# Filler counts and lane turns of the last loop in a four-layer decoder kernel

## What is computed

```python
x = _layernorm(x + _L2_attn_ref(x, ...))          # gated convolution
x = _layernorm(x + _L2_xattn_ref(x, ctx, ctx, ...))  # cross attention 0
x = _layernorm(x + _L2_ffn_ref(x, rhs))           # per-token int8 product
x = _layernorm(x + _L3_attn_ref(x, ...))          # retention
x = _layernorm(x + _L3_xattn_ref(x, ctx, mask, ...))
# cross attention 1, self attention and a gelu MLP, each with a norm
x = _layernorm(x + _L3_ffn_ref(x, ...))           # ternary MLP
# its body:
h = silu(tlin(x, w1, w1_s)) * tlin(x, w2, w2_s)
h = gelu(tlin(h, h1_w, h1_s), approximate=False)
h = gelu(tlin(h, h2_w, h2_s), approximate=False)
return tlin(h, w3_w, w3_s)
```

## Time and profile before

| | |
|---|---|
| median of 3 executions | 3279.0 us (3275.18 to 3295.63) |
| the profiled execution | 3275.2 us |
| its span | 3273.4 us |
| TensorE matmul busy | 2564.8 us, 78% of the span |
| VectorE busy | 1697.3 us, 52% |
| ScalarE busy | 987.1 us, 30% |
| GpSimd busy | 355.1 us, 11% |
| DMA | 15 GB/s on average |

### The profile page before, as it was taken

One profiled execution on the slowest core, in us unless ns is written; L12 is line 12 of the kernel. 1 busy time (PEld: TensorE's weight loads), 2 busy tenths in 40 slices (PEclk: granted clock), 3 DMA queues, 4 the chain that ended last, 5 costly groups with the idle time before them and its releaser, 6 DMA issues.

```text
span 3273.4 us, 52814 instructions
## 1 busy us (share of the span) xinstructions
PE 2564.8 (78%) x22974; PEld 1838.7 (56%) x22974; DVE 1697.3 (52%) x4037; ACT 987.1 (30%) x1377; POOL 355.1 (11%) x605
## 2 busy tenths in 40 slices
PE   4666568888888897786677779877798677987778
PEld 3444246777777776665555555555555455555554
DVE  5655744565656564522366541665416754166540
ACT  3333312223322231021232432324323243232431
POOL 0111100110011000055110000100001000010000
PEclk8888568999999999898899999989999999998999
DMA  2000000000000000225600000000000000000000
GB/s 84 1 1 1 2 1 1 8 8 2 8 8 8 8 1 8 96 32 85 163 1 1 1 7 1 1 1 1 7 1 1 1 1 7 1 1 1 1 1 26
DMA packets 39353, 48.12 MB, mean 15 GB/s; under 512 B 7169, under 2 KB 36369, under 8 KB 38354
## 3 DMA queue, kind: packets, MB, share of 16 engines
q1 hardware_dynamic: 33490, 40.43, 4.1%
q0 software_dynamic: 5632, 4.33, 1.0%
HBM read 31.81 MB, written 12.91 MB: 14 GB/s over the span
## 4 chain that ended last, share of the span: by engine, by line
PE 55%; DVE 31%; ACT 6%; issue 4%; POOL 3%; DMA 1%; SPq 0%; DVEq 0%; POOLq 0%; ACTq 0%
PE banks L2391 7%; PE banks L865 7%; DVE wide_area L2267 4%; PE banks L2590 3%; DVE wide_area L1745 3%; PE banks L1365 2%; PE banks L2165 2%; DVE weights L2084 2%; PE banks L1330 2%; PE banks L2380 2%; PE banks L1164 2%; DVE xs L894 2%; PE banks L1398 1%; PE banks L2174 1%; PE banks L1658 1%
## 5 line engine op out<-in xcount | busy, mean ns | idle before, releaser
L2590 PE MATMUL banks<-wA 128*128 128x128 f32 x2600 | 358.3, 291 | 4.2 <-ACT xf L926 2.1
L2590 PEld LDWEIGHTS banks<-wA 128*128 128x128 f32 x2600 | 331.8, 204 | 22.4 <-issue 15.1
L886 DVE BATCH_NORM_STATS2 stats<-banks 128x6 f32<-128x128 f32 x208 | 46.4, 286 | 406.7 <-PE banks L865 381.1
L2267 DVE TENSOR_REDUCE wide_area<-banks 128x8 f32<-128x2048 f32 x64 | 146.7, 2291 | 100.4 <-PE banks L2165 100.4
L901 POOL TENSOR_TENSOR rstd<-moments,eps 128x4 f32<-128x4 f32 x56 | 11.2, 199 | 1408.1 <-DVE moments L890 1408.1
L2248 ACT ACTIVATE weights<-banks 128x2048 f32<-128x2048 f32 x64 | 120.1, 1877 | 102.5 <-PE banks L2174 102.5
L1745 DVE TENSOR_REDUCE wide_area<-banks 128x16 f32<-128x1024 f32 x80 | 94.1, 1218 | 54.2 <-PE banks L1658 54.1
L886 DVE BATCH_NORM_STATS2 dilvals<-banks 128x6 f32<-128x128 f32 x144 | 32.1, 286 | 103.5 <-PE banks L865 103.5
L2391 PE MATMUL banks<-wide_area,big 128*128 128x512 f32 x192 | 85.0, 592 | 0.0
L894 DVE TENSOR_SCALAR xs<-banks,moments,rstd 128x128 f32<-128x128 f32 x208 | 70.8, 404 | 27.0 <-POOL rstd L903 25.5
L2084 DVE TENSOR_TENSOR weights<-banks,wC 128x2048 f32<-128x2048 f32 x32 | 72.2, 2287 | 22.5 <-PE banks L1971 22.5
(11 more groups left out here) (761 smaller groups left out, 6040.1 us busy)
## 6 DMA issues: line engine op xcount, KB each, us to landing
big<-in_wE SPq DMA_DIRECT2D x1, 4096.0 KB, 12.6
weights<-long_kernel SPq DMA_DIRECT2D x8, 512.0 KB, 7.1
conv<-wide_area SPq DMA_DIRECT2D x16, 256.0 KB, 2.5
wC<-in_wC SPq DMA_DIRECT2D x1, 3012.0 KB, 17.0
wC<-in_wG SPq DMA_DIRECT2D x1, 2971.0 KB, 19.3
big<-in_wT SPq DMA_DIRECT2D x1, 2560.0 KB, 11.6
x_all<-in_xT SPq DMA_DIRECT2D x1, 2048.0 KB, 10.4
total<-spread SPq DMA_DIRECT2D x8, 256.0 KB, 2.2
```

Of the source, the lines that this page charges most:

```text
L886: dve.bn_stats(m.stats[:, i, :], self.tokens(i)).then_inc(*sg.up("dve", f"stats{i}"))
L2267: return dve.tensor_reduce(m.peaks[:, k % 2, :, :].rearrange("p t (r c) -> p r t c", r=4)[:, :, :, SPARE[j]], m.bank[:, :, :].rearrange("p ...
L2590: pe.matmul(bank[:, 0:P], m.ident, m.ident, start=True, stop=True)
```

## The change

Two module constants change and nothing else. `BUSY` gets other filler counts at seven places of the last loop (its other entries are as they were, in another order), and `LAST` gets another order of the same 206 letters.

```diff
-BUSY = {..., 'last norm 0': 7, 'last norm 1': 13, 'last norm 2': 8, 'last norm 3': 9, 'last norm 4': 12, 'last norm 5': 7, 'last norm 8': 8, 'retention turned': 7, 'quant whole': 3, 'last norm 7': 2}
+BUSY = {..., 'last norm 0': 9, 'last norm 1': 12, 'last norm 2': 9, 'last norm 3': 12, 'last norm 4': 12, 'last norm 5': 8, 'last norm 7': 1, 'last norm 8': 8, 'retention turned': 7, 'quant whole': 2, ...}

-LAST = "nnfnnfnfnfnfnfnfnfnffnfnfnnfnffnnnfn...
+LAST = "nnfnnfnfnfnfnfnfnfnfnfnfnfnfnffnnnfn...
```

More of the change, by code:

```diff
@@ L808 @@
 MIDDLE = "nfnfnfnfnfnfnfnfnfnffnfnfnnfnnfnnnffffnfnffnffnn"
-BUSY = {'first1': 2, 'dil_sum0': 7, 'wide scores1': 8, 'lead norm': 10, 'near norm': 1, 'dil_peaks1': 12, 'dil_peaks0': 2, 'lead product': 5, 'wide start': 2, 'gate': 7, 'back0': 3, 'first3': 1, 'first0': 1, 'first norm': 6, 'taken': 20, 'chosen': 5, 'choice start': 8, 'choice same': 4, 'choice bit': 3, 'choice rank': 24, 'last norm 0': 7, 'last norm 1': 13, 'last norm 2': 8, 'last norm 3': 9, 'last norm 4': 12, 'last norm 5': 7, 'last norm 8': 8, 'retention turned': 7, 'quant whole': 3, 'last norm 7': 2}
-LAST = "nnfnnfnfnfnfnfnfnfnffnfnfnnfnffnnnfnffnfnfnfnfnfnfnfnfnfnfnfnnfnfnffnfnfnfnfnfnfnfnfnfnfnfnfnnfnfnffnfnfnfnfnfnfnfnfnfnfnfnfnfnfnfnfnfnfnfnfnfnfnfnfnfnfnfnfnfnfnfnfnfnfnfnfnfnnffnffnnfnffnfnffnnfnnfffnfnfnf"
+BUSY = {'first1': 2, 'dil_sum0': 7, 'wide scores1': 8, 'lead norm': 10, 'near norm': 1, 'dil_peaks1': 12, 'dil_peaks0': 2, 'lead product': 5, 'wide start': 2, 'gate': 7, 'back0': 3, 'first3': 1, 'first0': 1, 'first norm': 6, 'last norm 0': 9, 'last norm 1': 12, 'last norm 2': 9, 'last norm 3': 12, 'last norm 4': 12, 'last norm 5': 8, 'last norm 7': 1, 'last norm 8': 8, 'retention turned': 7, 'quant whole': 2, 'taken': 20, 'chosen': 5, 'choice start': 8, 'choice same': 4, 'choice bit': 3, 'choice rank': 24}
+LAST = "nnfnnfnfnfnfnfnfnfnfnfnfnfnfnffnnnfnffnfnfnfnfnfnfnfnfnfnfnfnnfnfnffnfnfnfnfnfnfnfnfnfnfnfnfnnfnfnffnfnnffnfnfnfnfnfnfnfnfnfnfnfnfnfnfnfnfnfnfnfnfnfnfnfnfnfnfnfnfnfnfnfnfnfnfnfnfnfnfnfnffnfnfnfnffnffnnfnnff"
 MIDDLE_ALONE = "nnnnf" * 6
```

## The result

| | before | after |
|---|---|---|
| median of 20 executions each | 3285.6 us | 3309.6 us |
| lowest to highest | 3275.2 to 3302.1 us | 3299.1 to 3326.8 us |
| the profiled execution | 3275.2 us | 3299.4 us |
| its span | 3273.4 us | 3297.6 us |

The changed kernel is slower: the ratio is 1.0083, with a 95% interval from 1.0067 to 1.0099. (This is the ratio on record for the executions of both kernels, and not the quotient of the two medians, which is 1.0073.

The account below looks back on a forecast made before the run. No engine is full; the path hops between engines with in-order queues, and the clock varies. Terms 1.8 + 6.4 + 0 - 2.5 = +5.7 us on a median of 3279.0 gave 3284.7, say 3285 us; range 3268 to 3302.

Parts of the forecast that it names:

- The fillers added: Norms 0, 2, 3, 5: only norm 2's extra fillers are on the path, 0.45 us per iteration, 1.8 us in all.
- The fillers removed: Norms 1, 7 and quant: 24 fillers taken where TensorE idles anyway, counted as nothing; bound -5.4 us.
- The start of self attention: Lane 0's scores ahead of lane 1's sum make L915 1.6 us late per iteration: 6.4 us, bounds 0 and 8.0.
- The idle times named as signs: Start of self attention: TensorE idle 0.85 us before lane 0's scores and 1.4 us before lane 1's L915 of norm 4.
- the second rival: New idle times before the scores and L915 bring clock falls, all iterations resembling iteration 3: +16 us, about 3300; chance 0.12.
- The feed-forward start: Lane 1's transposes fill a gap before lane 0's products, so clock falls may stay away: 0 to -5.1 us, taken -2.5.
- The ternary turns and the table loads: Ternary layer: two more table loads per iteration, 1.28 us each, hidden in ScalarE's waits: 0; unhidden 10.3 us.
- the faster one: Less idle before retention keeps the clock's upper level there in all iterations: 20.9 us won, 3266 as median; chance 0.10.
- the free attention move: Self attention: a later wait absorbs the moved scores' cost, 3285 - 6.4 = 3279 us; chance 0.15.
- a table load on the path: Ternary layer: one table load per iteration is not hidden, 1.28 us each, +5 us, 3290 us; chance 0.08.
- The size class: Whole kernel: change stays within about 1%, 33 us, of no change; same 0.93, faster 0.02, slower 0.05.

Follow-up runs that it names:

- before_norm7_one: The kernel before with norm 7's filler count set from two to one and nothing else; ratio 1.0002 to the kernel before, no difference.
- before_scores_moved: The kernel before with lane 0's first self attention scores moved ahead of lane 1's last sum and nothing else; ratio 1.0021, 7 us slower.
- scores_norm7: The kernel before with lane 0's first self attention scores moved ahead and norm 7's filler count at one; ratio 1.0029, 10 us slower.
- turns_norm7_one: The kernel before with all the new turns and norm 7's filler count at one, other counts as before; ratio 1.0039, 13 us slower.
- after_norm7_two: The changed kernel with norm 7's filler count put back from one to two; ratio 1.0038 to the kernel before, 12 us slower.
- scores_moved_filled: The kernel before with self attention's scores moved and lane 1's norm 4 filler count raised from 12 to 16; ratio 1.0004 to the kernel before.
- before_feed_moved: The kernel before with lane 1's transposes moved ahead of lane 0's four feed-forward products and nothing else; ratio 0.9995, no difference.
- after_delayed: The changed kernel with eight more fillers, once, ahead of lane 0's norm 2 in iteration 0; ratio 1.0062 to the kernel before, 20 us slower.

## Why the prediction was wrong

- **The fillers added** (1.8 us). Right as far as it can be seen: norm 2's block is longer and still followed at once by L915, and the projections behind it (L1939) start 3.15 us after the block's start instead of 2.92. The shortest stretch from L1610 to lane 0's L2192 took 185.6 us in the two kernels with the scores put back, and 185.0 to 185.1 in before, before_norm7_one, before_scores_moved and scores_norm7, which have eight fillers there: some 0.5 us, with the moves in cross attention 0 in it too, against the 0.45 forecast. But the added fillers also move all that follows, and no term of the sum held that. turns_norm7_one makes it likely, and does not prove, that the other counts matter in this way.
- **The fillers removed.** This is the step that failed. The text said "I give them nothing", because TensorE idles behind them and no engine waits. For norm 7 it had no row, only "the same form" as the quantised product's place. That they are on no path was right. It asked only what the removed work delays, not what the longer idle time does to the clock. Norm 7's fell from two to one, the idle time grew from 1.44 to 1.67 us, and the clock fell under the products behind it: 18.2 us in the trace, and some 15 us by after_norm7_two. The lower bound that the prediction took for these fillers, -5.4 us, had only their work in it.
- **The start of self attention** (6.4 us). The working was right to a tenth of a microsecond: 89.87 to 91.45 us where the clock holds, and lane 1's projections 1.59 us later behind lane 0's (2232.31 to 2244.57, against 2227.66 to 2238.33), with VectorE waiting for GpSimd's root. The idle times named as signs, 0.85 and 1.4 us, were 0.69 and 1.17. The fall that this wait brings, 1.7 us in each iteration, stood in the second rival and not in the sum. scores_moved_filled tells the two apart. That this stretch's net in the two traces, 6.6 us, is near the forecast's 6.4 is chance: 6.4 by the order, 6.7 by the new falls, and 6.4 less by the four old ones that went.
- **The feed-forward start** (-2.5 us of up to -5.1). All three falls went, so the bound was the value.
- **The ternary turns and the table loads** (0). Right: 77.60 before, 77.48 with the new turns at full clock, and the loads hidden. ScalarE's waits behind the loads were those of before. The Trainium skill (ScalarE: Activation LUTs, section "What ACT_TABLE_LOAD costs") counts a drain beside each load. The trace does not agree: the load at 2391.46 ends at 2392.74, and the silu behind it starts at 2392.75, 1.31 us after the gelu ahead of the load had ended. The layer was examined for its order and its table loads, and the loss in it came from a filler ahead of it.
- **The rivals.** The second one (the clock falls more, about 3300) had the right kind of mechanism and nearly the size: all iterations became about as long as the slow iteration 3. It had 0.12. The rival put the new falls at the start of self attention and in retention, and had none at the ternary layer. So its size was near by luck of the place: 18.2 us came in the ternary layer, which it did not name, and only 3.6 from the start of an iteration to self attention, retention included. The upper end of the range, 3302, was drawn about it, with the median of three executions as its base, which was 6.6 us too low; without that the result would be 3303.0, just outside. Of the others, the faster one did not come, since retention ran at the lower clock in places in every iteration, and neither did the free attention move nor a table load on the path.

  The Trainium skill, TensorE: Matmul & The Clock Gate, section "HAM oscillation — how this bites in real kernels", says that gaps bring the lower clock back, and that a loop stays at the full one where its work covers the waits. The runs with one, two and six fillers agree in kind, with 27 of 32, 10 of 28 and 0 of 20. They differ in size: the waits in the page's example are of some 3 to 5 us, and here the clock fell behind idle times of 1.67 and 1.17 us. The prediction set the page beside the earlier trace rows, which show the same 0.66 us of idle time ahead of a fall and ahead of none, and so speak neither way.
- **The size class** held: 0.83% lies within the 1% to which the text gave 0.93.

The reason why one filler costs some 15 us in the changed kernel and at most 4 in the one before is shown in part. Shown: how often and how deep the clock falls depends on the filler count and on what else stands in the loop; the changed kernel repeated one pattern in each iteration, in both executions profiled, from two different starts. Not shown: what in the other filler counts makes the pattern settle there.

## What to carry to other kernels

A product that computes nothing and delays nobody is not free to remove: where TensorE's idle time has been filled to hold its clock, read the granted clock of the stretch behind the fillers, iteration by iteration, before and after. In a loop whose iterations are a little unlike each other by the clock, judge an edit at full clock and at the lower one apart (the shortest window of a stretch tells the order, the others the falls), and time it in the whole kernel, since such effects neither add up nor carry over from one version to another. Fillers in a wait that no path crosses cost nothing here and protected the clock: put in more than just enough, and look whether what follows still starts when it did.

## What was not expected of the hardware

- The durations of a stretch come in steps. The ternary window took 77.5 or 77.6, 79.0 to 79.3, once 80.9, or 82.0 to 82.3 us in twenty profiles, and nothing between.
- 0.23 us more of idle time, 1.67 instead of 1.44, turned four iterations of four at full clock (after_norm7_two) into four with a fall (the changed kernel); in other versions of the loop the same step did less. With six fillers there was no fall in twenty iterations.
- The loop can lock: iterations of 409.60 to 409.69 us (before_feed_moved) and of 416.35 and 416.43 us (the changed kernel), with falls at the same distance from each iteration's start, while the kernel before spread over 9 us. The delay of after_delayed did not undo it. Other versions locked too: 413.04 and 413.03 us in after_norm7_two, 412.97 and 413.03 in scores_moved_filled.
- The kernel before had medians from 3277 to 3295 us on the six occasions, more than most of the effects here. Only the ratio to it on the same occasion tells anything.
